# The same units of an attention and expert kernel in another order on four engines

## What is computed

```python
x = x + xattn(_layernorm(x), ctx, ctx, Wq, bq, Wk, bk, Wv, bv, Wo, bo)   # x (16,64,256), ctx (16,1601,256)
x = x + attn(_layernorm(x), Wqkv, bqkv, Wout, bout)                      # with rotary positions
x = x + ffn(_layernorm(x), wg, W, b)                                     # 8 experts, 128 places each
# xattn: softmax(q k^T / 4) v for each head, then @ Wo.T + bo
# ffn:   expert = argmax(softmax(x @ wg)); a row over its expert's capacity gives 0
```

## Time and profile before

| what | value |
|---|---|
| runs | 701.28 us median of 3 (700.39 to 702.39) |
| profiled execution, span from first to last instruction | 699.7 us |
| TensorE busy | 671.0 us (96%) |
| GpSimd busy | 549.0 us (78%) |
| VectorE busy | 552.5 us (79%) |
| ScalarE busy | 443.4 us (63%) |
| DMA | 84.20 MB, mean 120 GB/s |

### The profile page before, as it was taken

One profiled execution on the slowest core, in us unless ns is written; L12 is line 12 of the kernel. 1 busy time (PEld: TensorE's weight loads), 2 busy tenths in 40 slices (PEclk: granted clock), 3 DMA queues, 4 the chain that ended last, 5 costly groups with the idle time before them and its releaser, 6 DMA issues.

```text
span 699.7 us, 21737 instructions
## 1 busy us (share of the span) xinstructions
PE 671.0 (96%) x8632; PEld 507.2 (72%) x8681; DVE 552.5 (79%) x1138; ACT 443.4 (63%) x885; POOL 549.0 (78%) x374
## 2 busy tenths in 40 slices
PE   4799999999999999999999999999999998899897
PEld 2556786877777877787778777877777786677673
DVE  4697877868888878778787868787868788888867
ACT  2446766666666666676767666767675787665830
POOL 7759999999699889798989789889788786723422
PEclk9999999999999999999999999999999999999999
DMA  8587055454445454545353645363543450000212
GB/s 309 143 213 214 27 138 162 99 155 97 150 113 155 105 164 92 160 107 165 93 165 84 178 102 159 85 187 89 169 97 104 100 164 4 2 2 9 91 69 91
DMA packets 45610, 84.20 MB, mean 120 GB/s; under 512 B 8668, under 2 KB 28420, under 8 KB 45508
## 3 DMA queue, kind: packets, MB, share of 16 engines
q1 hardware_dynamic: 43896, 80.13, 41.9%
q0 software_dynamic: 912, 2.14, 1.0%
q10 hardware_dynamic: 704, 0.55, 0.3%
HBM read 36.89 MB, written 6.55 MB: 62 GB/s over the span
## 4 chain that ended last, share of the span: by engine, by line
PE 82%; DVE 5%; DMA 5%; SPq 2%; issue 2%; POOL 2%; ACT 2%; ACTq 0%; DVEq 0%; POOLq 0%
PE ps_kv L821 17%; PE ps_kv L812 16%; PE ps_score L872 12%; PE ps_out L896 12%; PE ps_front L844 12%; PE ps_score L920 2%; SPq L502 2%; DMA kstack<-khigh 2%; PE ps_out L912 1%; DMA cbuf<-in_ctxT 1%; PE ps_kv L783 1%; DMA wq_sb<-in_wqT 1%; PE ps_front L920 1%; PE ps_front L853 1%; PE ps_kv L920 1%
## 5 line engine op out<-in xcount | busy, mean ns | idle before, releaser
L637 POOL TENSOR_TENSOR plow<-prob 128x1024 bf16<-128x1024 f32 (+1 forms) x198 | 372.1, 1898 | 58.8 <-ACT prob L1242 56.3
L1511 DVE TENSOR_REDUCE maxes<-ps_front 128x1 f32<-128x512 f32 (+1 forms) x416 | 267.1, 666 | 57.2 <-PE ps_front L844 53.9
L1242 ACT ACTIVATE prob<-ps_score 128x512 f32<-128x512 f32 (+1 forms) x416 | 236.2, 598 | 71.0 <-PE ps_score L872 61.9
L872 PE MATMUL ps_score<-qstack,kstack 98*128 98x128 bf16 (+1 forms) x1664 | 150.5, 219 | 0.8 <-ACT prob L1242 0.5
L844 PE MATMUL ps_front<-kstack,qstack 96*128 96x512 bf16 (+1 forms) x512 | 145.4, 333 | 2.7 <-DMA kstack<-khigh 1.9
L872 PEld LDWEIGHTS ps_score<-qstack,kstack 98*128 98x128 bf16 (+1 forms) x1664 | 112.1, 98 | 33.7 <-ACT prob L1242 1.9
L896 PE MATMUL ps_out<-vstack,prob 128*128 128x65 bf16 (+1 forms) x1664 | 113.6, 194 | 0.7 <-POOL plow L637 0.3
L821 PE MATMUL ps_kv<-w_hi,cbuf 128*128 128x256 bf16 (+1 forms) x402 | 109.7, 273 | 0.9 <-DVE vstack L1501 0.9
L1494 DVE SCALAR_TENSOR_TENSOR klow<-ps_kv,bcol,khigh 128x512 bf16<-128x512 f32 (+1 forms) x123 | 76.8, 629 | 42.5 <-ACT khigh L1220 42.0
L821 PE MATMUL ps_kv<-w_hi,clow 128*128 128x256 bf16 (+1 forms) x402 | 109.5, 272 | 0.0
L821 PE MATMUL ps_kv<-w_lo,cbuf 128*128 128x256 bf16 (+1 forms) x402 | 109.5, 272 | 0.0
(11 more groups left out here) (290 smaller groups left out, 858.7 us busy)
## 6 DMA issues: line engine op xcount, KB each, us to landing
kstack<-khigh SPq DMA_DIRECT2D x256, 100.1 KB, 2.2
cbuf<-in_ctxT SPq DMA_DIRECT2D x15, 1601.0 KB, 7.2
kstack<-klow SPq DMA_DIRECT2D x128, 100.1 KB, 2.2
qstack<-q_blocks SPq DMA_DIRECT2D x48, 64.0 KB, 2.3
q_blocks<-qbd SPq DMA_DIRECT2D x16, 128.0 KB, 2.0
cbuf<-in_weT SPq DMA_DIRECT2D x2, 1024.0 KB, 7.8
slot_x<-att_all SPq DMA_DIRECT2D x8, 128.0 KB, 7.1
vstack<-slot_x SPq DMA_DIRECT2D x4, 256.0 KB, 3.6
```

Of the source, the lines that this page charges most:

```text
L637: nc.gpsimd.tensor_tensor(plow[slot][0:n, :], prob[slot][0:n, :], p_high(slot, 0, HP * P)[0:n], ALU.subtract).then_inc(plow_gps, 1)
L872: mm = nc.tensor.matmul(ps_score[0:nn, h % NSB, j * P:(j + 1) * P], kstack[par][0:98, hp, n0:n0 + nn], qstack[par][0:98, q_at(hp), :], sta ...
L1242: nc.scalar.activation(prob[slot][0:nn, e * 512:e * 512 + 512], ps_score[0:nn, h % NSB, :], ACT.Exp)\
L1511: nc.vector.reduce_max(maxes[:, hp:hp + len(unit), n], ps[:, 0:len(unit) * nn].rearrange("p (h k) -> p h k", k=nn), AX.X).then_inc(m_free, 1)
```

## The change

The four strings are replaced by others with the same letters in the same numbers. Nothing else differs: the same units, instructions, waits, buffers and DMAs. No kind's own order changes; the interleaving does, over the whole program. The lines of the strings that hold the start and the end are these, and those between differ in the same manner.

```diff
 PE_PROGRAM = [
-    ("KKKKKKKKKKKKKmmKmmKmKmKmmKmKmKmmKmKmmmKKmmKmKmmKmKmmKKmmKmKmmsKmsmsKmsmsKmwsmswmwsKsmswmwwmKmsswmKwm"
+    ("KKKKKKKKKKKKmKmmKmmKmKmKmKmKmKmmKmKmmKmKmmKmKmmKmKmKmKmmKmKmsmKmmssKmmssKmmsswwmwsmsKmmsKwmsswwwmKsm"
 ...
-     "wwsmsKmsmsKwmmwsswmwwmswKwsmKmsmKmswsmmKmssmwwmwsmwswmsmKmwswsmwmsKmsmwswmsZmwswwsAwswwwwssOswsAwsww"
-     "ssOswswwswswsswwswssswsHsswwsJHswwsTJAVOTSVwwwwwSPPwHwwWJVAP2PTOoWSA2HOoJPPhVTHlWVJS2AToOhSPPhlWPl2"
-     "PHAocWOJAV2OHToJhSHhlTlVJcVPTPSWSPP2Wo2PPoxhWlxghcxglx2gcogFhFlFFFFcFFFFFF", 1),
+     "swmsmsKssmKwmmwKswsmwwwsmswmKmmsKmswmsmKsmmswwwmsmswwmsmKsmwwmsmsKsmwwmsmsZmwwwswsAwwsswwsOsAwswsws"
+     "sOwsswswwswsswswwwwswsHsswwsJHsswwsTJAVTOSVwwwSwwPPHwwwWJVP2ATPOoWSA2HOoJPPhVTHWlVJS2AToOShPPlhWlP2"
+     "PHAocWOJAV2OHToJShhlHlVTJcVPPTSSWPP2Wo2PoPxhWlxghcxg2lxgocgFhFFlFFcFFFFFFF", 1),
 ]
 ACT_PROGRAM = [
-    ("KKgKKKKKKKKKKKKKKgKKKKKKKKKKKKRKKReKeeeeKeKeeKeeKeeeeeeKKeeeeeeKeeReeKReeeKeKeeKeeKeeKeKeeKeKeeeegeK"
+    ("KgKKKKKKKKKKKKKKKgKKKKKKKKKKKKRKKReKeeKeeKeeeeeKKeeKeeeeKeeeeeeKeeReeKReeeKeKeeKeeKeeKeeKKeeKeeeegeK"
 ...
 DVE_PROGRAM = [
-    ("jKKKkKBzKkzKKCKmmmmmkmKmmjmmKmKmmKmKzmmKmKmmKmKmmKKmmKmKmKmKmmKmmmKmKmmmmKmKmmmmmKmmKmmmmmKmmKvKmmKm"
+    ("jkKKKzkKKBKzKKCmmmkmmmKmmjmmKmKmmKmKzmmKmKmmKmKmmKKKmmmKmKmKmmKmmKmmmmKmmKmKmKmmmmmmKmmmmmKmmKvKmmKm"
 ...
-     "KmKmmmKmaZpvppppXDXGDNpGLpNTLppTpXDGMMUUNaMMULUWvTXDxGWdNMgMLUUnXDGTNxLadgWTnMMUxUdXgDMnMUGUWN1xL3WX"
-     "DdGTNgXDLGxdngNTnMMLU1UT3MMUUWMMUUWxdgnxdqg1nqWq31qxd3gnyyyy1yyffy3fyyffyyy", 1),
+     "KmKmmmKmaZpvppXDppXGDpNGLpNLTppTpXDMGMUUaNMMULUWvTXDGxWdNMMgLUXUDnGxTNdLagWTnMMUxUdXgDMnMUUGWN1Lx3XW"
+     "DdGTNgXDLGxdngNTnMMUUL1T3MMUUMWUMUWxdgxndqg1nqW3q1qxdgn3yyy1yyfyfy3yyfyffyy", 1),
 ]
 POOL_PROGRAM = [
-    ("qcvccvvfqcfvvcvcvfccppppppppppppppppppccppcpcppppcpqppppfcpppcppcppppccpcppfpcpppppppppcppppppcppcpc"
+    ("cqvvcccvfqfvvvvccccfppppcpppppppppppppccppppcppppcqpppppfpcppcppcppppcppcppppcppcppfpppppcpcpppppppc"
 ...
-     "pcpcppppqpppppppcppcpccppppcpppcppcpppcpppppcppppppppccpcpppppppppppppppppbbpprrtZbptrbIbtbIIbrRrRbt"
-     "tRrrRtrsRsIsttssRRYYRggggYg", 1),
+     "pppccppppppppppcccpppcppppppcppppppcpccpppppppccpppcpppcppppppppppppppppppbbpprrtZbptrbIrbtRbbrRbRrt"
+     "ItIrtRsrtRsIsssRYRtYRgggggY", 1),
 ]
```

More of the change, by code:

```diff
@@ new lines @@
+    ("KKKKKKKKKKKKmKmmKmmKmKmKmKmKmKmmKmKmmKmKmmKmKmmKmKmKmKmmKmKmsmKmmssKmmssKmmsswwmwsmsKmmsKwmsswwwmKsm"
+     "swmKmssmwwwwmssmKsmswmwsmswmwsmsKmmwsswmwKmwwswswwswwsKmmsswwmKsmswKwmsmsKmswmswwwmKmmsKmswmKwmwsmsK"
+     "msswmwmswKwswmmsKmssmKswmwsmKwmwwsKmmwwKsmKsKmswswmwsmsKmmssKmwswsmwmwKswwmwmsKmmsKssmwwmwsmKsmswmww"
+     "mssKswmmwKsmsKmwwwmsmKmsmKmwswKwwmsKssKswwwmmKmswmsKmsmKswwmwswsmmKsKswKswsmKmswsmwwmKmwsmwswmKmmsKm"
+     "sswwmmswwsmwswKswmwsmKmwKmmKwwmwwswKsKssKsKssmmKmswsmwwmwsmsKmmwswwmwKmssKsmwswwmKsmmKmswswmwwssmwmK"
+     "msmwwsmsKmsKwmsKmmKmmwwwwsKwmwwKsKssKmmsKmswsmwmsKmsmwswwKmwssmKKswmKswmswwmwmwsKmsmKmmsKswswmwmsKsw"
+     "msmwKmsmwKmsmsKmmwKwwwsmwwKswwsKssmKmssmwKmsmswwwmsKsmswwmwmswKwsmwKmmssKmswsmKmwsmwwwmKmmsswKwwmssm"
+     "KmmKmssKmKwwwwsmmwKmsKwsswKmmssKwmssmKsmwswKsmwswmswKmsmwKmwmswwmsKmswKmmsKmsmKmwwmswsKwmswmwwssKmmw"
+     "ssKmsmKmmwKwswwwmwKsswwKsmsKsmmsKsmswwwwmsmwsKmsmwwsKwmswmsKmsmKmwwssmKswmmKmsmsKwmwKmssmwwwwsmmsKms"
+     "mKmmwwKwwswmwwKswsKssmmKmmssKmswswwwsKmsmKswwmswsKwmmwsswmKmswmwKmswsKmsmKmwsmKmwswmswKmwsmwsKmKmmKm"
+     "mwwwswKmwsKsKsswwKmmssKssmwwmwwsmwswsmmKsmwwswKsmKmmKsKmswmwsmsmKmwwmwsmwwKsmmKmsmsKswmwmsKmwssKwmww"
+     "mwKmsKssKswmwmsswKmwssmwwwsmsmKmsswKmwwsmwsmKwsKmwmKsmsKsmmsKmwwwmKswmwsmwKsmwmsKwmsmKmsmKmmwwKwswww"
+     "smKssKwwssKmsmswKmsmKmwsmwwsmwKwsmwsmKmsmswwmwswmwsKsmmKsmwsmwKmsmsKwmsmsKmmKwmmswKswKswwwmmwwKwmsKs"
+     "swwmmsKsmsKmsKsmwwswmmKwswswmmswsKsmswwmsmKmwswmmswsKmKmwswsmKwsmmKmwKsmmsKsswwmwKmwwKmmKsmwwKsmsmww"
+     "swmsmsKssmKwmmwKswsmwwwsmswmKmmsKmswmsmKsmmswwwmsmswwmsmKsmwwsmwmsKsmwwmsmsZmwwwswsAwwsswwsOsAwswsws"
+     "sOwsswwswsswswsswwwwswsHsswwsJHsswwsTJAVTOSVwwwSwwPPHwwwWJVP2ATPOoWSA2HOoJPPhVTHWlVJS2AToOShPPlhWlP2"
+     "PHAocWOJAV2OHToJShhlHlVTJcVPPTSSWPP2Wo2PoPxhWlxghcxg2lxgocgFhFFlFFcFFFFFFF", 1),
@@ L128 @@
 ]
 ACT_PROGRAM = [
-    ("KKgKKKKKKKKKKKKKKgKKKKKKKKKKKKRKKReKeeeeKeKeeKeeKeeeeeeKKeeeeeeKeeReeKReeeKeKeeKeeKeeKeKeeKeKeeeegeK"
[L131 to L138, removed]
+    ("KgKKKKKKKKKKKKKKKgKKKKKKKKKKKKRKKReKeeKeeKeeeeeKKeeKeeeeKeeeeeeKeeReeKReeeKeKeeKeeKeeKeeKKeeKeeeegeK"
+     "eeKeeKeKKReeKRKeeeeKeeKeeeKKeeeKeeKeeKeeeKeeeKKeKeReKeKeReKeKeKeeKeKeeeKeeKKeeKeeKeeKeeeegeeKKeeKRKR"
+     "KeeKeeKeeeKKeeeKeeKeeeeKeKeeeeKKeeKeKeeKRKKReKeKeeKeeKeeKeeKeKKeeKeeeKeKeeegeKeKeeeKeKRKReeKeeKeeKeK"
+     "eeeKeeeKeKeeKeeeKKeeKeKeKeKeKReKReKeeKeeeKeKeeeKeeKeKeKeeKeeKgeeeKeeKeKeRKeKReeKeKeeeeKeKeeeKeeKeKee"
+     "KeeKeKeKeKeeeeeKKRKReKeeeeKeKeeKeeKeeeKeKeKeeKeKeKeeegeKKeKeKReRKeKeeKeeeKKeeeeeKeeKeKKeeeKKeeeKKeeK"
+     "eeKeKeRKReKeeeKeeKeeeeKeeeKeKKeeKeKeKeegeKeeKeKKReeKReKeeKeeKeeKeKeeKeeeeKeeKeeKeKeeKeKKeeKKeeRReKee"
+     "KeKeeKeKeeeeKeeeKeeKeeeKKeeKeKKeeKKeRKeeRKeeeKeeeKeKKeeeeKeeKeeeKeeeZKeeeKeReeReeAeeeeeeAeeeeeeeeeee"
+     "eHeeeHeeeBATVBTVEEPPHEEV2APPTBA2HEEPPHfBiVTV2ABTEEfPPfiEiE2PHPlAAV2HBTffiHiVTlEBEVPBPTEPEP2EE2PPxhfi"
+     "xlyfhxy2ixlyyhfil", 1),
```

29 lines of the change are left out of this document (8 added, 21 removed).

## The result

The changed kernel takes 715.19 us (median of 6 runs, 714.16 to 718.50), the kernel before, beside it, 701.92 (700.39 to 702.57). The ratio is 1.0195 [1.0172, 1.0219]: 13.3 us slower, against a forecast of 702.0 and outside its range of 698.8 to 704.5. The profiled execution has a span of 713.7 us and took 715.71; its mean granted clock is 0.990, where that of before is 1.000.

A forecast was written before the change was run, and what follows sets the result against it. TensorE's own work was taken as the bound, busy 671.0 of 699.7 us. Start +1.1, middle 0 and end -0.4 gave +0.7, a span of 700.4; with 1.6 for the runs' median, 702.0 us, range 698.8 to 704.5.

The forecast's parts named there:

- After 606 the letters change places by one or two; 0.: Behind 606 us: units were said to move only one or two places in the strings, costing 0.
- The product behind the rotation: End, TensorE: a 1.08 us product no longer fills time ahead of a 1.1 us wait; costs 0.45, somewhat under half.
- VectorE's end, 0.85 to come back: End: units set into VectorE's waits at 580 and 586 us bring up to 1.4 us back; 0.85 taken.
- Start, +1.1: Before 80 us: TensorE leaves the start 1.1 us late, bounds -0.3 and +1.9.
- 0.9 ahead of 14.48: Start, ScalarE: the queries' part, now first, is ready at 13.55, so the queries are sent 0.9 us earlier.
- The wait of 1.44 that was to hide the later transpose: Start, TensorE: the wait for keys before the first row maxima at 29.16 hides a transpose 0.6 us later.
- the wait of 0.4 for the second one: Start: TensorE reaches the second low part of probabilities at 66.5, and it ends at 66.9; wait 0.4 us.
- Middle, 0, bound +0.8: From 80 to 562 us: the new order costs 0, bounds -0.5 and +0.8.
- four relations that were counted: Middle: TensorE work between score halves, bank and maxima, scores and weighing, shift copy and score half; only the last loses, 0.1.
- Waits of tenths of a microsecond batch after batch: Sign that the forecast would be wrong: TensorE waits of tenths of a microsecond coming back in batch after batch.
- The rivals: Faster: keys land 0.9 earlier and end holes fully used, 698.7, chance 0.18. Slower: late low parts, 704.4, chance 0.21.
- The four context quarters in a row: Slower rival, GpSimd: 4 x 1.52 us of quarters delay low parts of probabilities, together 2.4 us; 704.4, chance 0.21.

The follow-up runs named there:

- the start alone: The kernel before with the changed order up to about 81 us on all four engines: 702.10 against 702.03 us, ratio 1.0002.
- the two letters: The changed kernel with the first product put back ahead of the rotation on TensorE: 713.42 us against 701.15 for the kernel before, ratio 1.0155.

## Why the prediction was wrong, point by point

- **"After 606 the letters change places by one or two; 0."** This step failed, and it holds 9 to 10 of the 13.3 us. Behind 606 TensorE is not full, so there every unit's place against its producer counts, and the places were not looked at one by one, as they were for 571 to 606. GpSimd's second and third I do not change by one or two: they come eight and nine letters later in its string. What the runs showed in its place: 2.6 (put early in the changed kernel) to 4.8 (the trace's table, 606 to 650 us) for the ranking, and 4.6 for the last tiles.
- **The hold was in the trace of before, and was not weighed.** The norm takes 0.41 for the first tile in the earlier trace rows; for the second it took 2.29 at 589.50, in the kernel before already, and the two low parts of 2.90 took 4.42 at 593. A move on GpSimd was costed by GpSimd's own time, and not by what VectorE does beside it. The Trainium skill's rule named above spoke against GpSimd's part of this change.
- **The product behind the rotation, "somewhat under half, 0.45".** The sign was right, and the size not: 2.8 by the two letters. The wait went from 1.12 to 1.91, and the idle time brought the clock's fall (1.7), which was no part of any rival.
- **VectorE's end, 0.85 to come back.** The hole of 1.09 at 580 is gone, and the sum comes earlier among the low parts, as said. VectorE of the changed kernel:

```profile
580.17 2.35 DVE L1481 TENSOR_TENSOR plow<-prob 128x1024 bf16<-128x1024 f32 x2
582.44 0.42 DVE L1564 TENSOR_TENSOR klow<-ps_kv,x_all 128x256 f32<-128x256 f32 x1
```

TensorE's wait of 1.3 for the second tile's norm is gone, with 0.3 left for the first tile's (forecast near 0.5), and its lag of 2.4 at Z is 1.6 behind that norm: the 0.8 came back as forecast. But the next wait took it again: T is 2.3 late, since VectorE's two low parts at 595.28 took 4.50 beside GpSimd's.
- **Start, +1.1.** The lag in the trace is 0.86, within the bounds; by the runs, the start alone costs nothing that can be told (-0.6 to +0.8 us). The size came near by luck, since the way to it was another one. The queries' part on ScalarE began at 14.59, not 0.9 ahead of 14.48, because VectorE's scaling came 1.0 later. GpSimd's second query norm came 1.6 late instead of 0.6 (21.64 against 20.01), and so TensorE's transpose stood at 23.61 (forecast 22.6). Behind that wait of 3.56 the granted clock was 0.50 from 24.5 to 28 us, 1.7 us of work, which no term held. So TensorE reached the first maxima without any wait for keys, straight from its own units:

```profile
29.52 0.38 PE L844 MATMUL ps_front<-kstack,qstack 96*128 96x512 bf16 x1
```

The wait of 1.44 that was to hide the later transpose was used up. The first low part of probabilities began at 62.88 (forecast 63.1), and the wait of 0.4 for the second one did not come.
- **Middle, 0, bound +0.8.** Too low: 1.6 in the trace, 2 to 3 by the runs. (Of the kernel with the order of before from Z on, the profiled execution was the shortest, 702.76, and the others took 704.49 to 704.76; what they lose beyond the 1.6 is in no trace.) Of the four relations that were counted, three hold. The fourth, the score half behind the copy of the shift, was given "at most 0.1, once"; at 261.24 and 366.99 such a half starts 0.14 behind the end of that copy and 0.19 late. A fifth was not counted, a projection that takes over a bank whose low part VectorE must have fetched: the five late key units start about 0.15 behind the end of such a part. By the strings the TensorE work between the two shrinks, from 2.80 to 2.57 in one batch and 3.06 to 2.59 in another; that this is what makes them late is argued, not shown by a run. "Waits of tenths of a microsecond batch after batch" was the sign named for being wrong.
- **The rivals.** The four context quarters in a row did not make the low parts late: TensorE's wait for one from 80 to 562 is at most 0.4 in any trace with this middle on all four engines. The slower end came by another way, behind 606, and the range (to 704.5) held only what lies ahead of it.

## What to carry to other kernels

Where an order is changed over a whole program, go through the stretch in which the bounding engine already waits unit by unit: a full stretch forgives a move by a place, a tail of dependent units does not, and here 80% of the time made a quarter of the loss. When a unit moves on GpSimd, look at what VectorE does at its new time, and cost a short VectorE step like the ranking's or the norm at the length of the GpSimd instruction beside it. A wait of 2 us on TensorE may cost 1.7 more by the slower clock behind it, as it did here in most traces, and strings that were fitted to one another are tested together or not at all.

## What the runs showed of the hardware

- **The clock after short waits.** Behind the wait for the mask of 2.8 us, the granted clock fell to 0.50 in all six traces that have it (the changed kernel and five of the experiments). Behind the wait of 1.9 for the rotation, it fell in four of six; behind the waits of the last tiles (up to 1.7 or 1.9, with another of 0.9 to 1.2 near), in four of seven. In the traces where the waits for rotation and mask were 0.9 to 1.1, it did not fall. The stretch at 1.2 GHz was 3.4 us long, in three traces once 6.8, and cost half of that. The Trainium skill ("TensorE: Matmul & The Clock Gate", Part 1) says that the clock drops to 1.2 GHz after idleness and comes back only with sustained work; that agrees with what TensorE did before and after each of these stretches.
- **The hold can last through several instructions.** With the norm put first, VectorE's norm was held for 3.44, through a GpSimd low part (1.90) and three zero fills (1.05 for two and 0.56) that followed at once: it ended at 591.93, the last of these fills at 591.78. In the kernel before, the same norm ended at 591.79, behind fills that end at 591.64. In the kernel with GpSimd's letters spread it ended at 591.23, 0.15 behind a low part's end at 591.08, though the fills followed there as well. That a fill by itself holds a norm is seen in the changed kernel, where only one ran beside it (592.71 to 593.26) and the norm took 0.61 and ended at 593.40. Why the norm came in between low part and fills in one order and not in the other, no run here tells.
